# Values' product in the keys' transpose bank, keys' transposes ahead of the key and query block, VectorE's score masks first in its step

## What is computed

```python
x = x + linear_attention(layernorm(x))          # causal, 16 heads of 16
x = x + cross_attention(layernorm(x), ctx)      # 77 keys, one head, mask
x = x + ffn(layernorm(x))                       # shared expert + top-1 of 8 for 512 tokens

# linear_attention
q, k = relu(q) + 1e-6, relu(k) + 1e-6
kv  = cumsum(einsum('bhld,bhle->bhlde', k, v), axis=2)
num = einsum('bhld,bhlde->bhle', q, kv)
den = maximum(einsum('bhld,bhld->bhl', q, cumsum(k, axis=2)), 1e-6)
out = (num / den) @ out_w.T + out_b
```

## Time and profile before

| | us |
|---|---|
| median of 3 runs (399.4 to 399.86) | 399.58 |
| the profiled execution, its time | 400.33 |
| its span, first to last instruction | 398.5 |
| its mean granted TensorE clock | 0.993 |

### The profile page before, as it was taken

One profiled execution on the slowest core, in us unless ns is written; L12 is line 12 of the kernel. 1 busy time (PEld: TensorE's weight loads), 2 busy tenths in 40 slices (PEclk: granted clock), 3 DMA queues, 4 the chain that ended last, 5 costly groups with the idle time before them and its releaser, 6 DMA issues. The chain is left out here.

```text
span 398.5 us, 10545 instructions
## 1 busy us (share of the span) xinstructions
PE 372.2 (93%) x3489; PEld 265.7 (67%) x3489; DVE 297.6 (75%) x933; ACT 164.6 (41%) x396; POOL 277.4 (70%) x418
## 2 busy tenths in 40 slices
PE   8999899999999999999999999999889999989972
PEld 3575677777777777767777766777665756746751
DVE  2656777888878888888898787887555658799871
ACT  3172344454355344345534522524346544522310
POOL 5135857776667776677775677778869889486475
PEclk9999999999999999999999999999899999999998
DMA  7992691300210120031411003003000131019630
GB/s 235 334 272 66 176 322 37 77 19 15 45 39 19 27 65 16 16 67 37 152 35 47 16 19 78 13 17 80 15 16 27 52 120 54 0 57 312 198 137 15
DMA packets 38076, 33.32 MB, mean 84 GB/s; under 512 B 4425, under 2 KB 37224, under 8 KB 38024
## 3 DMA queue, kind: packets, MB, share of 16 engines
q1 hardware_dynamic: 35432, 28.68, 25.2%
q0 software_dynamic: 1456, 3.37, 2.9%
q10 hardware_dynamic: 1136, 0.60, 0.6%
HBM read 15.58 MB, written 13.78 MB: 74 GB/s over the span
## 5 line engine op out<-in xcount | busy, mean ns | idle before, releaser
L1519 POOL TENSOR_TENSOR s_t<-s_t,causal 128x512 f32<-128x512 f32 x64 | 80.9, 1286 | 22.9 <-ACT s_t L864 22.9
L487 PE MATMUL bank<-h1t,w_qkv 128*128 128x512 f32 x112 | 55.4, 617 | 1.9 <-DVE x L1099 1.9
L1511 POOL TENSOR_TENSOR state_wide<-state,own_pair 128x256 f32<-128x256 f32 x28 | 17.2, 613 | 35.1 <-DVE state L1089 33.0
L1135 DVE TENSOR_TENSOR s_t<-sbank,causal 128x512 f32<-128x512 f32 x64 | 40.8, 679 | 0.0
L546 PE MATMUL bank<-s_t,vp 128*32 128x128 f32 x1024 | 35.6, 280 | 3.0 <-DVE s_t L1135 1.0
L864 ACT ACTIVATE s_t<-sbank 128x512 f32<-128x512 f32 x64 | 34.2, 588 | 9.1 <-PE sbank L508 9.0
L494 PE MATMUL bank<-w_qkv,h1t 128*128 128x256 f32 x128 | 35.9, 403 | 2.2 <-DVE arena L1055 2.1
L508 PE MATMUL sbank<-arena 32*128 32x256 f32 x512 | 37.3, 406 | 0.0
L1099 DVE TENSOR_TENSOR x<-bank,x 128x256 f32<-128x256 f32 x32 | 13.6, 425 | 29.3 <-PE bank L625 29.2
L718 PE MATMUL sbank<-h1t,w 128*128 128x512 f32 x72 | 33.1, 598 | 1.9 <-DVE block_hot L1395 1.4
L625 PE MATMUL bank<-w_out,attn_t 128*128 128x256 f32 x128 | 33.3, 383 | 0.0
(11 more groups left out here) (215 smaller groups left out, 844.0 us busy)
## 6 DMA issues: line engine op xcount, KB each, us to landing
rden_t<-rden SPq DMA_DIRECT2D x64, 64.0 KB
rows<-x SPq DMA_DIRECT2D x32, 128.0 KB, 1.7
x<-in_x SPq DMA_DIRECT2D x7, 512.0 KB, 7.4
out<-x SPq DMA_DIRECT2D x7, 512.0 KB, 4.8
we<-in_we SPq DMA_DIRECT2D x1, 2048.0 KB
rows<-empty SPq DMA_DIRECT2D x1, 1419.0 KB, 6.3
rows<-empty SPq DMA_DIRECT2D x1, 1408.0 KB, 7.5
xmask<-in_mask POOLq DMA_DIRECT2D x2, 616.0 KB, 6.5
```

Source lines behind the costliest of these rows:

```text
L487: mm = pe.matmul(dst[:, :], w_qkv[:, ch, cb * P:(cb + 1) * P], h1t[:, g % 3, ch, :], start=(ch == 0), stop=(ch == CH - 1))
L1135: dve.tensor_tensor(s_t[:, r, :, :], sbank[r][:, :].rearrange("p (s q) -> p s q", s=4), causal[:, :].unsqueeze(1).to_broadcast([P, 4, P]), ...
L1519: pool.tensor_tensor(s_t[:, r, :, :], s_t[:, r, :, :], causal[:, :].unsqueeze(1).to_broadcast([P, 4, P]), ALU.mult)\
```

## The change

Four edits, all in the loop of steps:

- The values of tile t (all but t = 0) are computed into the upper half of `bank[2]`, not the lower half of `bank[0]`. Their product waits for ScalarE's copy of this step's `k_tok` (which reads the lower half), no longer for the eviction of the block and for x.
- The keys' transposes go ahead of the block on PE. They and the denominators, which write `bank[2]` too, now wait for the values' eviction.
- The output product, the next to write `bank[0]` after the block, waits for the block's eviction in place of that of the values.
- VectorE masks its two score banks at the beginning of its step, ahead of x, not between the block's eviction and that of the values.

```diff
+        def v_place(t):
+            return bank[2][:, D:2 * D] if t else bank[0][:, 0:D]
@@ PE: values
-                    mm = pe.matmul(bank[0][:, 0:D], h1t[:, (t // GT) % 3, ch, tok(t)], w_qkv[:, ch, 2 * D:3 * D],
+                    mm = pe.matmul(v_place(t), h1t[:, (t // GT) % 3, ch, tok(t)], w_qkv[:, ch, 2 * D:3 * D],
@@ PE: denominators
                 wait(pe, ktok_ready, GT * g + 1)
+                wait(pe, v_ready, GT * g + 2)
@@ PE: step
-                if g < NG:
-                    wait(pe, x1_ready, i - 1)
-                    wait(pe, v_ready, i + 1)
-                    qk_block(g, i % GT, bank[0])
-                if i > NT:
-                    gate_products(pe, i - NT - 1, 0)
                 if is_tile(K):
                     wait(pe, qk_ready, 4 * (K // GT) + 2)
                     wait(pe, ktok_ready, K)
                     wait(pe, den_ready, -(-K // GT))
+                    wait(pe, v_ready, K + 1)
                     for ch in range(CH):
                         mm = transpose(bank[2][:, ch * P:(ch + 1) * P], kt((K // GT) % 2, ch)[:, tok(K)])
                     mm.then_inc(ktr_done, 1)
+                if g < NG:
+                    wait(pe, x1_ready, i - 1)
+                    qk_block(g, i % GT, bank[0])
+                if i > NT:
+                    gate_products(pe, i - NT - 1, 0)
...
                 if is_tile(V):
-                    wait(pe, qk_ready, min(4 * NG, 4 * g + i % GT + 1))
-                    wait(pe, x1_ready, i - 1)
+                    wait(pe, ktok_ready, K + 1)
                     values(V)
...
                 if is_tile(M):
                     wait(pe, attn_ready, M + 1)
-                    if is_tile(V):
-                        wait(pe, v_ready, V + 1)
+                    wait(pe, qk_ready, min(4 * NG, 4 * g + i % GT + 1))
@@ DVE: v_evict
-                dve.tensor_tensor(v_of, heads(bank[0][:, 0:D]), heads(b_v[:, :]), ALU.add).then_inc(v_ready, 1)
+                dve.tensor_tensor(v_of, heads(v_place(t)), heads(b_v[:, :]), ALU.add).then_inc(v_ready, 1)
@@ DVE: step
                 g = i // GT + 1
+                if is_tile(M):
+                    mask_scores(M, 2, 4)
                 if is_tile(X1):
                     wait(dve, out_done, X1 + 1)
...
                 if g < NG:
                     qk_evict(4 * g + i % GT, bank[0])
-                if is_tile(M):
-                    for r in range(2, RG):
-                        wait(dve, s_done, M + 1)
-                        wait(dve, num_done, M)
-                        dve.tensor_tensor(s_t[:, r, :, :], sbank[r][:, :].rearrange("p (s q) -> p s q", s=4),
-                                          causal[:, :].unsqueeze(1).to_broadcast([P, 4, P]), ALU.mult)\
-                            .then_inc(s_masked, 1)
```

More of the change, by code:

```diff
@@ L1091, in new_state, with mask_scores @@
                             .then_inc(state_ready, 1)
+            def mask_scores(t, lo, hi):
+                for r in range(lo, hi):
+                    wait(dve, s_done, t + 1)
+                    wait(dve, num_done, t)
+                    dve.tensor_tensor(s_t[:, r, :, :], sbank[r][:, :].rearrange("p (s q) -> p s q", s=4),
+                                      causal[:, :].unsqueeze(1).to_broadcast([P, 4, P]), ALU.mult)\
+                        .then_inc(s_masked, 1)
             def step(dve, i):
```

## The result

The changed kernel takes 397.16 us in the median of 13 runs (396.14 to 399.02) against 399.86 for the kernel before on the same chips (398.73 to 401.34): ratio 0.9939, interval 0.992 to 0.9957. It is faster by 0.6%, 2.4 to 2.7 us. The forecast was 392.8, range 390.6 to 396.8: the sign was right, the gain less than half of the forecast, and the time outside the range.

The account below looks back on a forecast made before the run. PE bounds the loop's steps with a key and query block, VectorE close behind. Part 1 -8.04, parts 2 and 3 +2.42, steps 28 to 32 -1.12 sum to -6.74: from 399.58 to 392.8 us, range 390.6 to 396.8.

Parts of the forecast that it names:

- the values' stall: On PE, the values' product waits for VectorE's eviction of the key and query block; removing it gains 8.67 us.
- parts 2 and 3: Keys' transposes before the block on PE, masks before x on VectorE; costed together as a loss of 2.42 us.
- theory 1: From the experiments: VectorE instructions reading two SBUF tiles and GpSimd instructions reading SBUF hold each other up when they meet.
- one behind a reciprocal: Steps after 4k: the denominators' reciprocal leaves VectorE a 0.43 hole; masks delay x by 0.70, parts 2 and 3 cost +0.48.
- one behind a split: Steps 17, 21, 25: bias splitting fills VectorE's hole; masks delay x by 1.20, parts 2 and 3 cost +0.98 each.
- steps 28 to 32: VectorE's earlier masks stop delaying the numerators: 0.6 in steps 28 to 30, 0.52 in step 32, together -1.12 us.
- what is late next: Waits once the values' stall is gone: k_tok copy has 1 us cover, GpSimd's masks 2.1; 0.63 given back.
- part 1: Values computed in the other bank, so their wait for the block's eviction goes: -8.67 + 0.63 = -8.04 us.
- Rival D: Gain partly eaten: VectorE's or GpSimd's queue later than assumed in more steps; 395 to 398; 15%.
- Rival A: PE's clock fall after 286.88, costing about 1.6 us: absent, 391.2 (12%); a second one, 394.4 (8%).
- Rival B: VectorE's masks slowed in their new slot beside ScalarE's copies; 406 at 0.25 us per mask; 5%.
- Rival C: Values still wait, now for ScalarE's k_tok copy; the 8.67 is lost, time 401.5; 3%.

Follow-up runs that it names:

- the run without the bias: Changed kernel with GpSimd adding the output bias to 1 of 256 features only: 392.68 us, ratio 0.9799 to the kernel before.
- masks in the middle: Changed kernel with VectorE's masks between the statistics and the block's eviction: 393.50 us, ratio 0.981 to the kernel before.
- fills: Changed kernel with 16 small GpSimd fills, which read nothing, replacing the bias addition except for 1 of 256 features: 395.44 us, ratio 0.9859 to before.
- masks back: Changed kernel with VectorE's masks back between the block's eviction and that of the values: 400.50 us, ratio 0.9993 to the kernel before.

## Why the prediction was right or wrong

**Right: the values' stall.** 8.67 was forecast for 28 steps. In ordinary steps 1.54 became 1.32 (0.22, forecast 0.23), in steps 24 to 27 1.76 became 1.31 (0.45, as forecast), and no step's values wait for the block. ScalarE's copy of k_tok is never late, as said.

**Right: parts 2 and 3 cost more than they give.** The steps behind a split of biases show it plainest: no hole, masks of 1.29, then x (step 17 after, compare):

```profile
166.83 0.69 DVE L1318 TENSOR_TENSOR be_rest<-be 72x512 f32<-72x512 f32 x1
167.55 1.29 DVE L1101 TENSOR_TENSOR s_t<-sbank,causal 128x512 f32<-128x512 f32 x2
168.75 0.41 DVE L1114 TENSOR_TENSOR x<-bank,x 128x256 f32<-128x256 f32 x1
```

Where theory 1's meeting is taken away, most single steps come out as forecast: a step without delay -0.35 to -0.42 (forecast -0.37), an ordinary one -0.35 (-0.31), one behind a reciprocal +0.18 (+0.25), one behind a split +0.75 in step 21 (+0.75); these are differences of the scores' starts between before and the run without the bias. The sum of the stretch was 5.4, the run gave 6.0. Two things that I left out nearly cancel. Steps 9, 17 and 25 are the second tile of a sequence: no state part stands there between values and numerators, so before the change the numerators waited for VectorE's masks, and now they don't (0.51, 0.28 and 0.29 more than forecast, 1.1 in all). In the step behind each of them VectorE's chain is late and x with it (0.33 less than forecast, 1.0 in all). The 0.6 is mostly x in ordinary steps: it was delayed 0.11 and not 0.14, and PE was the later, 0.04 a step.

**Right: steps 28 to 32.** In steps 28 to 30 the numerators follow the state part by 0.54 for 0.74, and in step 32 by 1.13 for 1.65, which are the 0.6 and 0.52 forecast. The meeting took 0.26 of it back in step 28 (longer by 0.06, in the run without bias shorter by 0.20).

**Wrong: "what is late next".** That step of part 1 named ScalarE's copy, GpSimd's masks and VectorE's masks. It did not look at VectorE's way from the values over the attention output to x, because I held its durations fixed and so put at nothing what PE's gain costs there: whatever PE gains, sums and products start earlier by as much and take what they took. They don't. In the changed kernel the sums are 0.14 longer in the median than before and 0.26 longer than undisturbed. This reached PE by two ways. Mostly VectorE's list as a whole was later, and with it masks, x and block: of the 3.4 us that the meeting cost in the stretch about 2.8 came so, up to 0.33 in a step. The rest are steps 8, 16 and 24, 0.2 each, where the output product was late for the attention output and the block behind it. In before the output product began 0.17 behind the transpose in every step of the stretch; now it does so later in eight. In step 9, without a state part, it shows most:

```profile
106.03 1.51 DVE L1072 TENSOR_TENSOR_SCAN arena<-arena,zero 128x512 f32<-128x512 f32 x1
107.46 0.39 DVE L1179 TENSOR_TENSOR attn_t<-bank,rden_t 128x256 f32<-128x256 f32 x1
```

```profile
107.41 0.34 PE L479 MATMUL bank<-ident,prob 128*77 128x128 f32 x1
107.91 1.13 PE L629 MATMUL bank<-w_out,attn_t 128*128 128x256 f32 x4 [0.16 <-DVE attn_t L1179]
```

The output product starts half a microsecond behind the transpose at 107.41, for the attention output that a sum of 1.51 had put off; without the bias it is still 0.28.

Removing the meeting is worth 3.4 us in the stretch, more than the 2.8 by which the stretch missed its forecast. Of the 4.0 us by which the whole gain fell short, the meeting is thus 3.4 and the 0.3 of step 28, and the longer time outside the span, which the sum carried over from before without a reason, about 0.8; the 0.6 above goes against them. Rival D had the range of the outcome (395 to 398) at 15%. That VectorE's queue is later in more steps is what happened, but the causes that it named were others: it knew of no instruction that gets longer. The stated range closed at 396.8, and the outcome lies just beyond it.

The trace of before already told: the products were 685 in the median and 853 at most, the sums 1199 to 1432, in bands, while every mask took 657 to 684. A band in an instruction of fixed size has a reason, and I looked at it only for the masks. Set beside the overlap with the addition, the durations of before, changed and masks in the middle fall in line: in steps 5 to 23 a sum took 1.36 to 1.38 with 0.3 us of overlap, 1.50 to 1.52 with 0.43, 1.59 to 1.60 with 0.52 and 1.72 to 1.74 with 0.65, so it lost the overlap less about 0.15 against its shortest 1.22. The Trainium skill, SBUF — State Buffer, section "Who interferes with whom", states the rule: a VectorE instruction with two SBUF inputs contends with a GpSimd instruction that reads SBUF, not with one that only writes, and an instruction with one SBUF input does not. The runs agree in all three parts (sums 1.25 beside fills, up to 1.74 beside the addition, masks 0.63 to 0.69 in any place), the second of them with fills that write little.

**Rival A, the clock.** It was a condition of every single run, not a rival between the kernels. Of 23 runs of the kernel before beside the first experiments, those at a mean clock of 0.997 had spans of 396.5 to 396.8 us and those at 0.983 of 399.2 to 399.6, the same program. The changed kernel had 393.6 at 0.997, in executions taken at another time. Of the ten profiled executions, four have a fall between 280 and 287 us (before, changed without bias, masks back, masks in the middle) and six have none there. So the fall that I priced at 1.6 us comes and goes, and the spans at equal clock differ by about 3.0. The Trainium skill's free-running window (TensorE: Matmul & The Clock Gate, Part 1) fits that; no run here shows what sets the moment of a fall.

**Rival B** did not happen: no mask of the changed kernel, 56 of the 64 beside ScalarE's copies of the other score banks, took over 0.69. **Rival C** did not happen. The side that B was to price, slower than before, exists elsewhere: masks first without the values' new bank is 2% slower.

## What to carry to other kernels

When an edit speeds up one engine, list what the other engines' instructions will then run beside, and look in the trace whether an instruction of fixed shape has more than one duration: that band can be the price of a meeting, and here it grew with the overlap. Of an edit in parts, each part's place can be judged against the holes only after the other parts have moved them: here masks in the hole before x were a loss of 2% alone, and after the values had left the block's bank the hole before the block's eviction was free for them and the better place. Compare one stretch at equal clock before comparing spans.

## What the runs showed of the hardware

- VectorE's running sum over 128x512 with two SBUF inputs took 1.20 to 1.29 us undisturbed and up to 1.74 beside GpSimd's 128x256 addition (0.74 us); its product up to 1.22 for 0.69. The loss was the overlap less about 0.15 us. A 72x8 VectorE addition of 0.16 us took 1.25 when it began 0.04 us behind a GpSimd mask of 1.25.
- A GpSimd addition of one element per partition took 0.19 us alone and up to 1.06 when it began inside such a sum; small fills beside the sum delayed nothing. An addition over 256 elements that began 0.08 inside a sum took 1.72 for 0.74, and the sum its undisturbed 1.28.
- VectorE's masks, one input from PSUM and one from SBUF, were not slowed by GpSimd's 128x512 masks or ScalarE's copies of other banks (0.63 to 0.69 us over all 64 of the changed kernel, 42 of them beside GpSimd's masks and 56 beside such copies).
- The same program's span varied by 3 us with the mean granted clock (0.997 to 0.983).
- A product whose weights were not loaded ahead, since it waited for VectorE, had a first matmul 0.10 us longer (0.697 for 0.595 us, 128x512).
- The time outside the span was 1.8 us in every execution of the kernel before and 2.4 to 3.0 in all 13 of the changed one; the cause is open.
